# Two adapters' B through one turn, one rounding and one split, in a loop body of sixteen pairs

## The reference

```python
w, b = weights[subjects], bias[subjects]
x = x + einsum('bct,bcd->bdt', x, w) + b[:, :, None]
H = einsum('btd,od->bto', x, W)
xa = einsum('btd,brd->btr', x, A[adapter_idx])
delta = einsum('btr,bor->bto', xa, Bm[adapter_idx]) * scalings[adapter_idx]
x = x + H + delta
```

## Time and profile before

| what | value |
|---|---|
| median of 3 runs | 244.95 us (244.68 to 245.31) |
| profiled execution, its own time | 244.87 us |
| its span, first to last instruction | 243.2 us |
| mean granted clock of TensorE | 0.995 of full speed |
| busy | PE 95%, PEld 78%, DVE 62%, ACT 45%, POOL 30% |
| DMA | 36.56 MB, mean 150 GB/s |

### The profile page before, as it was taken

One profiled execution on the slowest core, in us unless ns is written; L12 is line 12 of the kernel. 1 busy time (PEld: TensorE's weight loads), 2 busy tenths in 40 slices (PEclk: granted clock), 3 DMA queues, 4 the chain that ended last, 5 costly groups with the idle time before them and its releaser, 6 DMA issues.

```text
span 243.2 us, 9842 instructions
## 1 busy us (share of the span) xinstructions
PE 231.2 (95%) x2916; PEld 189.1 (78%) x2917; DVE 149.7 (62%) x259; ACT 108.8 (45%) x189; POOL 73.2 (30%) x280
## 2 busy tenths in 40 slices
PE   1989999999999999999999999999999999999991
PEld 1767888888888888888788888888888888888760
DVE  6688866675367836675368736675368754525662
ACT  2175373563526353463525445353526434344431
POOL 3466601560046300651036400656324141000000
PEclk9999999999999999999999999999999999999998
DMA  6745564745555573645546464655547364642333
GB/s 135 265 143 152 160 187 120 213 116 171 152 152 161 140 215 87 202 121 174 159 130 184 128 196 122 189 125 162 161 143 199 94 198 116 201 130 67 84 71 88
DMA packets 23621, 36.56 MB, mean 150 GB/s; under 512 B 6066, under 2 KB 6066, under 8 KB 23602
## 3 DMA queue, kind: packets, MB, share of 16 engines
q1 hardware_dynamic: 16544, 26.36, 39.1%
q10 hardware_dynamic: 7058, 9.97, 13.9%
HBM read 19.53 MB, written 16.78 MB: 149 GB/s over the span
## 4 chain that ended last, share of the span: by engine, by line
PE 89%; DVE 5%; DMA 2%; issue 1%; ACT 1%; POOL 0%; SPq 0%; DVEq 0%; ACTq 0%; POOLq 0%
PE ps L859 69%; PE ps L828 13%; PE ps L804 3%; DMA x_ring<-in_x_dram 2%; PE ps L873 1%; PE ps L877 1%; PE ps L763 1%; DVE x_lo L527 1%; DVE m_lo L510 1%; DVE x L519 1%; PE ps L798 0%; DVEq L60 0%; SPq L237 0%; DVE b_parts L491 0%; DVE o_ring L547 0%
## 5 line engine op out<-in xcount | busy, mean ns | idle before, releaser
L859 PE MATMUL ps<-m_hi,x_hi 128*128 x248 | 99.0, 399 | 0.0
L859 PE MATMUL ps<-m_hi,x_lo 128*128 x248 | 96.8, 390 | 0.0
L859 PE MATMUL ps<-m_lo,x_hi 128*128 x248 | 96.7, 390 | 0.0
L527 DVE TENSOR_TENSOR x_lo<-x,x_hi 128x512 fp32r<-128x512 f32 x64 | 44.2, 691 | 62.2 <-ACT x_hi L645 62.0
L368 POOL COPY p_pair<-p_all 64x64 f32 x128 | 40.4, 316 | 124.9 <-DVE x L519 86.6
L645 ACT ACTIVATE x_hi<-x 128x512 fp32r<-128x512 f32 x64 | 40.4, 632 | 54.0 <-ACT o_ring L658 30.0
L658 ACT ACTIVATE o_ring<-ps 128x512 f32<-128x512 f32 x60 | 35.8, 597 | 56.0 <-PE ps L859 55.8
L859 PEld LDWEIGHTS ps<-m_hi,x_hi 128*128 128x128 f32 x248 | 46.5, 188 | 10.4
L859 PEld LDWEIGHTS ps<-m_hi,x_lo 128*128 128x128 f32 x248 | 46.6, 188 | 10.1
L859 PEld LDWEIGHTS ps<-m_lo,x_hi 128*128 128x128 f32 x248 | 46.6, 188 | 9.1
L519 DVE TENSOR_TENSOR x<-ps,bias_pair 128x512 f32<-128x512 f32 x64 | 43.7, 685 | 7.9 <-PE ps L828 7.0
(11 more groups left out here) (99 smaller groups left out, 82.7 us busy)
## 6 DMA issues: line engine op xcount, KB each, us to landing
x_ring<-in_x_dram SPq DMA_DIRECT2D x124, 128.0 KB, 2.7
out_dram<-o_ring ACTq DMA_DIRECT2D x64, 128.0 KB, 2.7
out_dram<-o_ring SPq DMA_DIRECT2D x64, 128.0 KB, 2.3
a_f<-in_L_cond_A_dram SPq DMA_DIRECT2D x8, 128.0 KB
o_ring<-in_L_cond_W_dram SPq DMA_DIRECT2D x2, 256.0 KB, 4.5
o_ring<-in_L_cond_W_dram ACTq DMA_DIRECT2D x2, 256.0 KB, 5.7
x_ring<-in_x_dram ACTq DMA_DIRECT2D x4, 128.0 KB, 3.2
b_nat<-in_L_cond_Bm_dram ACTq DMA_DIRECT2D x1, 256.0 KB, 3.8
```

The costliest lines, as they stand in the source:

```text
L527: nc.vector.tensor_tensor(x1_lo[:, u % HELD], x1[:, u % 2], x1_hi[:, u % HELD], ALU.subtract).then_inc(x1_lo_ready, 1)
L859: mm = nc.tensor.matmul(ps[:, 2 + u % 2, :], part, m_tile(m, k, c), start=(c == 0 and part is hi and m is m_hi), stop=(c == TC - 1 and par ...
```

## The change

The loop has 3 bodies of 16 pairs in place of 6 bodies of 8, and each body makes two M from one turned B. GpSimd writes the B of the first of the two adapters into columns 0 to 63 and that of the second into columns 64 to 127 of `b_dup`; one `turn_b`, one `b_round` and one `b_split` handle both. `a_f` has 128 rows and `a_parts` two halves: the first adapter's A lies in rows 0 to 63 of half 0, the second's in rows 64 to 127 of half 1, with zeros in the other rows, so that each product takes its own adapter from the common `b_parts`. The four copies of a row now lie side by side (row 4r+g where it was 16g+r), which lets `neg` be computed on VectorE from two bits of the row number. The zeros of `a_parts` are written by GpSimd instead of VectorE. The two loads of A, two `a_round` and two `a_split` of a body stand one behind the other. `tiles_of` and `sums_of` keep the products and sums at the same pairs as before.

```diff
-    BODY = 8
-    BODIES = 6
+    BODY = 16
+    BODIES = 3
...
-        a_f = sb("a_f", [GR, T])
-        a_parts = sb("a_parts", [P, T], F32R)
+        a_f = sb("a_f", [P, T])
+        a_parts = sb("a_parts", [P, 2, T], F32R)
...
+        def half_of(u, n):
+
+            return 0 if n is None or HEAD + 2 <= u < HEAD + 6 else 1
...
-                sp.dma_start(a_f[:], A[ds(k, 1)].to_broadcast([G, R, T])).then_inc(a_in, 16)
+                sp.dma_start(a_f[GR * half:GR * half + GR, :], A[ds(k, 1)].rearrange("k r t -> r k t").to_broadcast([R, G, T])).then_inc(a_in, 16)
...
-                    load_a(n + 2)
+                    for half in range(2):
+                        load_a(n * 2 + (2 + half), half)
...
-            nc.gpsimd.memset(neg[:], 0.0).then_inc(consts, 1)
-            pool.wait_ge(consts, 7)
-            nc.gpsimd.affine_select(out=neg[:, 0:1], in_=neg[:, 0:1], compare_op=ALU.is_gt, fill=-1.0,
-                                    base=2 * R, pattern=[[0, 1]], channel_multiplier=-1).then_inc(consts, 1)
...
+            pool.wait_ge(consts, 6)
+            for half in range(2):
+                nc.gpsimd.memset(a_parts[GR - GR * half:P - GR * half, half, :].bitcast(F32), 0.0).then_inc(rows_zeroed, 1)
+                pool.wait_ge(rows_zeroed, half + 1)
...
                 if n is not None and u == 7:
-                    dup_b(n + 2)
-                    pool.wait_ge(b_dupped, n + 3)
+                    for half in range(2):
+                        dup_b(n * 2 + (2 + half), n + 2, half)
+                    pool.wait_ge(b_dupped, n * 2 + 4)
...
+            bits = [did(nc.vector.tensor_scalar(bits_i[:, part:part + 1], pid_i[:], 2 - part, None, ALU.bitwise_and))
+                    for part in range(2)]
+            need(bits[1])
+            for part in range(2):
+                nc.vector.tensor_scalar(neg[:, part:part + 1], bits_i[:, part:part + 1], -0.5 - 0.5 * part, None,
+                                        ALU.mult).then_inc(zeroed, 1)
...
-            nc.vector.memset(a_parts[GR:P, :].bitcast(F32), 0.0).then_inc(zeroed, 1)
...
                 if n is not None and u == HEAD + 1:
-                    a_split(n + 2)
+                    for half in range(2):
+                        a_split(n * 2 + (2 + half), half)
                     b_split(n + 2)
...
                 if n is not None and u == HEAD:
-                    a_round(n + 2)
+                    for half in range(2):
+                        a_round(n * 2 + (2 + half), half)
                     b_round(n + 2)
...
                 if not isinstance(i, int):
-                    pe.wait_ge(m_added, i * TC - 1 - TC)
...
+                    pe.wait_ge(b_dupped, i * 2)
+                    pe.wait_ge(m_added, i * (2 * TC) - (3 * TC + 1))
...
-                if n is not None and u == HEAD + 2:
-
-                    pe.wait_ge(m_ready, n * TC + 2 * TC)
+                if n is not None and u in (HEAD + 2, HEAD + 10):
+
+                    pe.wait_ge(m_ready, n * (2 * TC) + (2 + half_of(u, n)) * TC)
```

More of the change, by code:

```diff
@@ L53, in cond_residual_layers @@
     HEAD = 4
-    BODY = 8
-    BODIES = 6
+    BODY = 16
+    BODIES = 3
     TAIL = HEAD + BODY * BODIES
-    assert PAIRS == 64 and BODIES == K - 2 and TAIL % 4 == 0 and TAIL <= PAIRS - MIXED
+    assert PAIRS == 64 and 2 * BODIES == K - 2 and TAIL % 4 == 0 and TAIL <= PAIRS - MIXED
     with ExitStack() as ctx:
@@ L154, in cond_residual_layers @@
         zeroed = sem("zeroed")
+        rows_zeroed = sem("rows_zeroed")
         p_ready = sem("p_ready")
@@ L214, in pairs @@
                 for u in range(BODY):
-                    step(n * BODY + (head + u), (head + u) % 8, n)
+                    step(n * BODY + (head + u), (head + u) % BODY, n)
             for j in range(head + BODY * BODIES, PAIRS):
@@ L344, in dup_b @@
                     pool.wait_ge(scal_ready, 1)
-                at_least(pool, b_turned, i)
-                nc.gpsimd.tensor_tensor(b_dup[:, :, 0:G, :],
+                at_least(pool, b_turned, turns)
+                nc.gpsimd.tensor_tensor(b_dup[:, :, R * half:R * half + R, :],
                                         b_nat[:, ds(k, 1), :].rearrange("p k (c r) -> p (k c) r", c=TC)
-                                        .unsqueeze(2).to_broadcast([P, TC, G, R]),
-                                        scal_all[:, ds(k, 1)].unsqueeze(2).unsqueeze(3).to_broadcast([P, TC, G, R]),
+                                        .unsqueeze(3).to_broadcast([P, TC, R, G]),
+                                        scal_all[:, ds(k, 1)].unsqueeze(2).unsqueeze(3).to_broadcast([P, TC, R, G]),
                                         ALU.mult).then_inc(b_dupped, 1)
             pool.wait_ge(order_ready, 1)
-            dup_b(0)
+            dup_b(0, 0)
             pool.wait_ge(b_dupped, 1)
@@ L480, in _, with a_split, b_split @@
                                   .rearrange("a (j h) -> a j h", h=2)).then_inc(others_ready, 1)
-            def a_split(i):
+            def a_split(i, half=0):
                 dve.wait_ge(a_rounded, i + 1)
[L485 to L491, removed]
+                rows = slice(GR * half, GR * half + GR)
+                nc.vector.scalar_tensor_tensor(out=a_parts[rows, half, :], in0=a_parts[rows, half, :], scalar=neg[rows, 0:1],
+                                               in1=a_f[rows, :], op0=ALU.mult, op1=ALU.add).then_inc(a_ready, 1)
+            def b_split(turn):
+                dve.wait_ge(b_rounded, turn + 1)
+                nc.vector.scalar_tensor_tensor(out=b_parts[:], in0=b_parts[:], scalar=neg[:, 1:2], in1=b_turned_at(turn),
                                                op0=ALU.mult, op1=ALU.add).then_inc(b_ready, 1)
@@ L616, in _, with a_round, b_round @@
             nc.scalar.activation(x1[:, 0, 0, 0:1], ones[:, 0:1], ACT.Copy).then_inc(warmed, 1)
[L617 to L627, removed]
+            def a_round(i, half=0):
+                act.wait_ge(a_in, 16 + i * 16 if isinstance(i, int) else i * 16 + (2 - half) * 16)
+                at_least(act, m_summed, i * TC - half * TC)
+                rows = slice(GR * half, GR * half + GR)
+                nc.scalar.activation(a_parts[rows, half, :], a_f[rows, :], ACT.Copy).then_inc(a_rounded, 1)
+            def b_round(turn):
+                act.wait_ge(b_turned, turn + 1)
+                at_least(act, m_summed, turn * TC if isinstance(turn, int) else turn * (2 * TC) - 2 * TC)
+                nc.scalar.activation(b_parts[:], b_turned_at(turn), ACT.Copy).then_inc(b_rounded, 1)
             def m_round_first(chunk):
@@ L797, in m_product_first, with m_product @@
                     pe.wait_ge(wt_copied, chunk)
-                nc.tensor.matmul(ps[:, FIRST + chunk, :], a_parts[:, chunk * P:chunk * P + P], b_parts[:],
+                nc.tensor.matmul(ps[:, FIRST + chunk, :], a_parts[:, 0, chunk * P:chunk * P + P], b_parts[:],
                                  start=False, stop=True, skip_group_check=True).then_inc(m_summed, 1)
-            def m_product(t, chunk):
+            def m_product(t, chunk, half):
                 at_least(pe, m_added, t - TC - 1)
-                nc.tensor.matmul(ps[:, 4 + chunk % 2, :], a_parts[:, chunk * P:chunk * P + P], b_parts[:],
+                nc.tensor.matmul(ps[:, 4 + chunk % 2, :], a_parts[:, half, chunk * P:chunk * P + P], b_parts[:],
                                  start=True, stop=True).then_inc(m_summed, 1)
```

44 lines of the change are left out of this document (20 added, 24 removed).

## The result

The changed kernel takes 243.28 us (median of 6 runs, 243.04 to 243.73), the kernel before 245.02 (244.68 to 245.31): ratio 0.9928, 95% interval 0.9907 to 0.9948. The forecast was 243.2 us in a range from 242.6 to 244.7, and faster. The profiled execution took 243.22 us, with a span of 241.5, 1.7 less than before.

The account below looks back on a forecast made before the run. The prediction took PE (TensorE) to bound the kernel, with 89% of the chain. Three turns (1.47 us) plus the prologue (0.25 us) save 1.72 us: 244.87 - 1.72 = 243.15, forecast 243.2 us, range 242.6 to 244.7.

Parts of the forecast that it names:

- Turns taken away: TensorE's loop: three of six turns of B go, each 0.44 + 0.05 = 0.49 us of the chain, saving 1.47 us.
- the bound of 1.7: Upper bound in us on the turns' saving, if the 0.13 us between two eight-pair stretches goes with bodies, not chance.
- Work taken from and put together on ACT and DVE: ScalarE and VectorE in the loop: fewer `b_round` and `b_split`, longer bursts; counted as zero, up to 1.37 us per body without cover.
- The cover: Room between the end of `b_split` and the first product reading it: 3.3 us before, more than 2 us expected after.
- The loop itself: Loop control: three back edges fewer, worth nothing as branches are hidden; the doubled body's code was the one risk.
- The rival: TensorE's two taken back edges fetch code no longer held: up to 10.6 us exposed in all; slow case, chance 0.07.
- the middle case of 4: Code-fetch rival with 2 us exposed at each back edge: 243.2 + 4 = 247.2 us; slow case, chance 0.07.
- The prologue: Before the loop: `a_parts` memset leaves VectorE, `onehot` comes 0.3 to 0.4 us earlier, 0.25 us reaches the end.
- The sum: Whole kernel: 1.47 from the turns plus 0.25 from the prologue, 1.72 us saved.
- the main term: The three turns taken from TensorE in the loop, 1.47 us.

Follow-up runs that it names:

- turn_twice: The changed kernel with each of the loop's three turns sending its four transposes twice: 244.56 us, ratio 0.9968 to the kernel before.
- zeros_on_gpsimd_before: The kernel before with only the memset of `a_parts` moved from VectorE to GpSimd: 246.13 us against 245.56 on that chip, ratio 1.0011.
- a_order_alone: The kernel before with only A's copies reordered, each row four times in a row, B left in its old order: 244.70 us against 244.86, ratio 0.9981.
- the other two comparisons: The unchanged changed kernel timed against the kernel before on two more chips: 243.12 us, ratio 0.9892, and 243.44 us, ratio 0.9930.

## Why the prediction was right

**Turns taken away.** Right, a little less than 3 x 0.49 = 1.47. The loop got 1.28 us shorter, and turn_twice puts 1.3 us back in the profile. A turn is 0.43 to 0.44 us, and the 0.05 us that was added to it for the pairs behind isn't seen when it is doubled (5.45 us behind eight transposes, 5.49 behind four). The rest, 1.32 to 1.28, is within what some layer 0 of four pairs vary: 2.15 us instead of 2.02 in three places of that stretch after, in two before. In the changed kernel they stand at the same place of each body; why is open. The 0.13 us between two stretches of the earlier trace rows, from which the bound of 1.7 was made, isn't the price of a body either: 0.08 of it comes from the first window's end, 80.00, where the next layer 0 starts at 79.92.

**Work taken from and put together on ACT and DVE.** Zero, as said. The cover is thinner than forecast: `b_split` ended 1.8, 1.5 and 1.6 us ahead of the first product in the three bodies, not more than 2, since the burst ends 1.8 us later behind its turn than in the earlier trace rows, where 1.37 was the most that was reckoned with; the product keeps its place behind the turn:

```profile
95.68 0.75 DVE L498 SCALAR_TENSOR_TENSOR b_parts<-b_parts,neg,ps 128x512 fp32r<-128x512 f32 x1
...
97.95 0.39 PE L816 MATMUL ps<-b_parts,a_parts 128*128 128x512 f32 x1
```

**The loop itself.** Right in the loop: no back edge mattered, and sixteen pairs are held. The rival was real and near. At 24 pairs one edge exposes 1.89 us; two such edges would have been 3.8 us, close to the middle case of 4, and the change would have been slower. But "fewer of them are worth nothing" leaves out what the longer body does behind the loop: 0.4 us less in the last stage, in every profile of a kernel with one. Why is open.

**The prologue.** This is the step that was wrong: its 0.25 us did not reach the end, and its mechanism was another. "All that follows, down to the first x load, hangs on `onehot`" fails: with `onehot` at 3.38 or sooner, A's issue stays at 6.30 to 6.34 behind ScalarE's table (zeros_on_gpsimd_before). What brought the first layer 0 forward, by 0.85 us, was in the main A's row order, which the prediction named only as a risk (a_order_alone: 0.99 us at the first layer 0, 1.7 us at A). And it isn't passed on: GpSimd's layouts for pair 7, which the prediction didn't look at, hold layer 0 of pairs 4 to 7, and 0.09 us is left at the third turn, which is less than one kernel varies there.

**The sum.** Of the 1.72 us forecast, the three turns gave 1.3 and the prologue nothing that can be told. The 0.4 us of the last stage, which the sum put at nothing, made up the difference. The way and the main term were right for the reason given; that the median met 243.2 so closely is luck, two errors of about 0.4 us against each other, and the other two comparisons have 2.44 and 1.42 us.

## What to carry to other kernels

Count what leaves the saturated engine and read its place in the chain; nearly all of that came through, and nearly nothing of an earlier start did, since a second engine (here GpSimd) had its own due time a little further on. Before a prologue gain is put in the sum, follow it to the next point where another engine must be done, and see what holds that one. A loop body may be doubled while no code arrives on the later walks, and a body a half longer still can fall off the edge: look at the code queues' blocks, in the first walk, in the later ones and behind the loop.

## What the runs showed of the hardware that was not expected

- The same 128 KB of A, read as each row four times in turn instead of all sixteen rows four times, are issued in 0.61 to 0.62 us instead of 0.70 and land at 9.7 to 10.8 us instead of 10.8 to 11.7; the read of a batch's number behind the issue takes 545 to 556 ns instead of 846 to 1019 (ten profiles and four). Why isn't shown.
- TensorE walks a body of sixteen pairs (717 matmuls and 717 weight loads) again without a block arriving, though eight had arrived in the first walk, neighbouring code included; of a body of 24 pairs nine blocks arrive again.
- The last stage, whose code no edit touches, takes 8.77 to 8.84 us behind a loop of eight-pair bodies and 8.29 to 8.44 behind longer ones (three profiles and eleven). Two blocks of code arrive on q14 in it in the first case, none in the second; that they are the cause isn't shown.
- GpSimd's small copies grow from 0.23 to 1.08 us beside VectorE's operations on two operands in SBUF, and end 0.09 us after them.
